# State-space scans on one Trainium2 core: the fourth channel block's input products by ScalarE and TensorE, and two of four scans in place in their PSUM banks

## The reference, cut to what matters

```python
def _mamba(x, in_w, conv_w, conv_b, xproj_w, dt_w, dt_b, A_log, D_param, out_w):
    xz = x @ in_w.T
    xh, z = jnp.split(xz, 2, axis=-1)
    ...                                  # causal conv of 4 taps, silu -> xc
    proj = xc @ xproj_w.T                # dt (16), Bm (16), Cm (16)
    delta = jax.nn.softplus(dt @ dt_w.T + dt_b)
    A = -jnp.exp(A_log)
    deltaA = jnp.exp(jnp.einsum('bld,dn->bldn', delta, A))
    deltaBu = jnp.einsum('bld,bln->bldn', delta * xc, Bm)
    def step(h, inp):
        dA, dBu, c = inp
        h = dA * h + dBu
        y = jnp.einsum('bdn,bn->bd', h, c)
        return (h, y)
    ...
    y = ys.transpose(1, 0, 2) + xc * D_param
    return (y * jax.nn.silu(z)) @ out_w.T
```

## Time and profile before

| | before |
|---|---|
| median of 3 runs | 5116.01 us (5112.91 to 5116.14) |
| profiled execution: its time, its span | 5119.58 us, 5117.9 us |
| mean granted TensorE clock | 0.935 |
| scans of all 16 halves | from 1144 to 2868 us of the span |
| busy in the whole span | PE 87%, DVE 68%, ACT 43%, POOL 48% |
| busy from 1253 to 2759 us (14 halves) | POOL 1431 of 1506 us, DVE 1354, PE 1245, ACT 855 |

### The profile page before, as it was taken

The page is one execution under the profiler, slowest core; times in us unless marked ns, Lnnn a source line. Parts: engine busy times, 40 slices in busy tenths (PEclk is TensorE's granted clock), DMA queues, the critical chain, the costliest instruction groups (busy, mean ns, idle before and its releaser), DMA issues. The chain is left out here.

```text
span 5117.9 us, 65289 instructions
## 1 busy us (share of the span) xinstructions
PE 4445.0 (87%) x22600; PEld 2900.7 (57%) x22600; DVE 3499.4 (68%) x7168; ACT 2189.7 (43%) x4132; POOL 2460.3 (48%) x1575
## 2 busy tenths in 40 slices
PE   7888599948888888888888799997898899999999
PEld 4555487623333333333333345796344799999998
DVE  4664222248988989889898574311896788888885
ACT  3555011125555555555555454333664233333332
POOL 3442400059999999999999441000122133222332
PEclk8998799969999999999999799998999899999999
DMA  2002213332222222222222100374000100000000
GB/s 73 1 1 97 79 52 109 100 99 70 70 70 70 68 68 70 69 70 70 69 70 70 39 1 7 132 263 159 1 1 18 71 5 3 5 5 5 5 5 5
DMA packets 153112, 287.22 MB, mean 56 GB/s; under 512 B 24441, under 2 KB 135024, under 8 KB 144206
## 3 DMA queue, kind: packets, MB, share of 16 engines
q1 hardware_dynamic: 144926, 263.59, 15.7%
q0 software_dynamic: 6656, 14.04, 0.9%
q10 hardware_dynamic: 1200, 5.42, 0.3%
HBM read 252.33 MB, written 33.42 MB: 56 GB/s over the span
## 5 line engine op out<-in xcount | busy, mean ns | idle before, releaser
L1734 PE MATMUL ssm_ps<-ssm_hc,net_ident 128*128 128x452 f32 x2048 | 950.8, 590 | 197.3 <-DVE ssm_hc L1990 105.4
L1916 POOL TENSOR_TENSOR ssm_dBu<-ssm_du,ssm_bc 128x904 f32<-128x904 f32 x512 | 1067.3, 2110 | 3.2 <-POOL ssm_du L1934 1.9
L1835 ACT ACTIVATE ssm_ps<-ssm_step,ssm_decay 128x448 f32<-128x448 f32 x1024 | 647.8, 636 | 651.1 <-DVE ssm_ps L1980 438.1
L1734 PEld LDWEIGHTS ssm_ps<-ssm_hc,net_ident 128*128 128x128 f32 x2048 | 387.9, 202 | 729.8 <-issue 341.3
L1980 DVE TENSOR_TENSOR_SCAN ssm_ps<-ssm_ps,ssm_dBu 128x452 f32<-128x452 f32 x512 | 565.2, 1104 | 132.9 <-POOL ssm_dBu L1916 46.0
L1980 DVE TENSOR_TENSOR_SCAN ssm_hs<-ssm_ps,ssm_dBu 128x452 f32<-128x452 f32 x512 | 551.4, 1077 | 40.2 <-ACT ssm_ps L1835 35.7
L1927 POOL TENSOR_TENSOR ssm_hc<-ssm_hs,ssm_bc 128x904 f32<-128x904 f32 x256 | 539.8, 2109 | 73.9 <-DVE ssm_hs L1980 73.8
L3170 POOL TENSOR_TENSOR peer_hid<-peer_hid,peer_weight 128x452 f32<-128x452 f32 x256 | 288.7, 1168 | 525.7 <-ACT peer_weight L3120 525.7
L3035 PE MATMUL peer_ps<-peer_xn,peer_down 128*128 128x226 f32 x2048 | 439.3, 361 | 0.0
L3101 PE MATMUL peer_ps<-peer_hid,peer_up 128*128 128x226 f32 x2048 | 398.8, 355 | 2.7 <-POOL peer_hid L3170 2.2
L3101 PEld LDWEIGHTS peer_ps<-peer_hid,peer_up 128*128 128x128 f32 x2048 | 388.2, 190 | 11.2 <-POOL peer_hid L3170 4.1
(11 more groups left out here) (425 smaller groups left out, 8000.9 us busy)
## 6 DMA issues: line engine op xcount, KB each, us to landing
ssm_bc<-ssm_rows SPq DMA_DIRECT2D x256, 452.0 KB, 3.6
l_ff_w<-in_l_ffn_w SPq DMA_DIRECT2D x64, 1024.0 KB, 6.7
moe_w_gu<-in_moe_gate_up SPq DMA_DIRECT2D x16, 704.0 KB
slots_in<-rt_zeros SPq DMA_DIRECT2D x17, 640.0 KB, 8.5
moe_rows_in<-slots_in SPq DMA_DIRECT2D x16, 512.0 KB
slots_out<-xp_rows_out SPq DMA_DIRECT2D x16, 512.0 KB
moe_w_dn<-in_moe_down SPq DMA_DIRECT2D x16, 384.0 KB
peer_down<-in_peer_down_t SPq DMA_DIRECT2D x1, 4096.0 KB, 16.3
```

The costliest lines, as they stand in the source:

```text
L1734: nc.tensor.matmul(Y_BANK[j][:, 0:GT], c["ident"][:, :], hc[:, q % 2, j, :], start=False, stop=(n == S - 1))\
L1835: nc.scalar.activation(rows(dA(i % 2))[:, :, lo:lo + N - 1], rows(step[hf.d][:, j, :])[:, :, lo:lo + N - 1], ACT.Exp, scale=decay[hf.d][:, ...
L1916: nc.gpsimd.tensor_tensor(dBu[:, q % 2, j:j + 2, :], du[hf.d][:, j:j + 2, :], bc[:, q % RING, 0:1, :].to_broadcast([P, 2, GT]), ALU.mult). ...
```

## The change

1. **Block 3's input products** leave POOL, for 15 of 16 states. The next half's B rows are turned once (tokens on partitions, `bT`, PE at slot 49 and ACT at slot 50), and so is block 3's `du` (`duT`, PE at slot 1, ACT at slot 3). Then ACT scales `duT` by a column of `bT`, one row of 113 tokens at a time (4 copies of 113x128 per state, `scaledT`), and PE turns the four results back into the bank `T_BANK`, which was `HS_BANK`. For n = 0 POOL still makes the product, in an instruction of its own (128x452), into `scaledT`. POOL's second input product is now block 2 alone (128x452).
2. **The scan of block 3** runs in place in `T_BANK` (for n = 0 in `scaledT`, in SBUF); its decays go to an SBUF tile, `dA_late`. **The scan of block 2** runs in place in its decay bank.
3. Since block 2's scan overwrites the zeros of bank 1, ACT zeroes them once a step with a small copy (`zeroed`), ahead of that slot's Exp.
4. `yz` now shares the buffer `conv`, with two new waits for that.

```diff
+    BT_MM, BT_OUT, DUT_MM, DUT_OUT = 49, 50, 1, 3
+    def turn_at(n):
+        return 6 if n == 1 else 50 if n == 12 else 4 * n + 1
+    def scale_at(n):
+        return (4, 4, 5, 5) if n == 1 else tuple(4 * n - 2 + b for b in range(4))
...
+        def dA(i):
+            return dA_late[:, :] if i % IB == LAST else A_BANK[i % 2][:, 0:GT]
+        def terms(hf, n, j):
+            q = S * hf.r + n
+            if j < LAST:
+                return dBu[:, q % 2, j, :]
+            return whole(hf, n) if n == 0 else T_BANK[:, 0:GT]
+        def late_state(hf, n, j):
+            return dA(AT[j]) if j < LAST else terms(hf, n, j)
...
+                    def turn_terms(hf, n):
+                        at = turned_before(hf, n)
+                        pe.wait_ge(s["hc_dve"], 2 * (S * hf.r + n))
...
+                        for b in range(GB):
+                            pe.wait_ge(s["scaled_done"], GB * (at - 1) + b + 1)
+                            mm = nc.tensor.transpose(T_BANK[:, b * N:(b + 1) * N], scaledT[0:N, n % 2, b, :], c["ident"][0:N, 0:N])
+                        mm.then_inc(s["turned_mm"], 1)
...
                     def decays(hf, i):
                         n, j = i // IB, ORDER[i % IB]
-                        if i >= 2:
-                            act.wait_ge(s["scan_done"], SLOTS * hf.r + i - 1)
+                        q = S * hf.r + n
+                        if i % IB == 1:
+                            if q:
+                                act.wait_ge(s["hc_dve"], 2 * q - 1)
+                            nc.scalar.activation(starts(i, hf.d), one[:, :].unsqueeze(1).to_broadcast([P, GB, 1]), ACT.Copy, scale=0.0)\
+                                .then_inc(s["zeroed"], 1)
+                        elif i == 0 or i == LAST:
+                            act.wait_ge(s["starts_zero"], 2 * hf.r + (1 if i == 0 else 2))
                         else:
-                            act.wait_ge(s["starts_zero"], 2 * hf.r + i + 1)
+                            act.wait_ge(s["scan_done"], SLOTS * hf.r + i - (3 if i % IB == LAST else 1))
...
+                                nc.scalar.activation(scaledT[0:N, n % 2, b, :], duT[:, b, :], ACT.Copy,
+                                                     scale=bT[:, hf.r % 2, b, n:n + 1]).then_inc(s["scaled_done"], 1)
...
-                        nc.gpsimd.tensor_tensor(dBu[:, q % 2, j:j + 2, :], du[hf.d][:, j:j + 2, :],
-                                                bc[:, q % RING, 0:1, :].to_broadcast([P, 2, GT]), ALU.mult).then_inc(s["dbu_done"], 1)
...
+                        nc.gpsimd.tensor_tensor(dBu[:, q % 2, 2, :], source[:, 2, :], row, ALU.mult).then_inc(s["dbu_done"], 1)
+                        if n == 0:
+                            if hf.r:
+                                pool.wait_ge(s["turned_mm"], turned_before(hf, 0))
+                            nc.gpsimd.tensor_tensor(whole(hf, 0), source[:, LAST, :], row, ALU.mult).then_inc(s["first_last"], 1)
...
                         if j >= 2:
-                            state = HS_BANK[:, 0:GT]
-                            if 2 * q + j - 2 > 0:
-                                dve.wait_ge(s["hc_dve"], 2 * q + j - 2)
+                            state = late_state(hf, n, j)
+                            if j == 2:
+                                dve.wait_ge(s["zeroed"], q + 1)
```

105 lines of the change are left out of this document (88 added, 17 removed).

## The result

The changed kernel takes 5080.40 us (median of 4 runs, 5077.52 to 5082.43), the kernel before 5116.08 beside it (4 runs, 5112.91 to 5119.00). The ratio is 0.9935, with a 95% interval of 0.9923 to 0.9947: faster by 36 us, where 50 were predicted. The profiled execution took 5081.52 us. Nearly the whole gain lies in the scans: in the profiled executions it is 1722.0 us from the start of the first to that of the last before, and 1687.1 after. Over the 14 middle halves a half takes 108.48 us before and 106.67 after. (My window of the earlier trace rows was 1506 us, a little less than the 1518.8 of 14 halves, so its figures per half were 0.8% low.)

A forecast was written before the change was run, and what follows sets the result against it. POOL and DVE were taken as near their limit in turn. Per half 4.6 + 1.4 - 0.5 - 0.7 - 1.7 = 3.1 us, 50 us in all, gave about 5070, or 5066 as median; own range 5026 to 5101, over all 4990 to 5128.

The forecast's parts named there:

- What bounds the kernel: POOL and DVE hand the limit back and forth; taking work from POOL alone returns at most 2.9 us a half.
- Own wait: Scans behind 23 of 32 DVE products a half stop waiting 0.20 us each: 4.6 us gained, bounds 0 and 7.
- POOL: DVE's waits for POOL shrink: 1.4 us a half gained, bounds 0 and 2.9.
- Slot 1: Where halves meet, POOL's product gets 0.9 to 1.0 us shorter; some 1.5 of the 2.5 us wait stays.
- The other waits: DVE's remaining waits for POOL, 2.9 - 2.5 = 0.4 us a half, go.
- ACT: Copies and zeroings raise ACT from 61 to about 83 of 104 us; -0.5 and +0.35 at SILU slots, put at 0.
- PE and the turn: Block 3's chain of product, add and turn has 1.1 us slack, broken at OUT_MM: 0.5 us a half lost.
- The signs to look for: In the profile after, new DVE waits for PE's turn appear in few slots (13 and 51), not every step.
- STEP: At slots 48 to 51 ACT stands behind B's turn with its copy and LOG; STEP about 0.7 us late.
- Two SBUF inputs: For n = 0, block 3's scan and product contend with POOL, 0.8 to 0.9 each: 1.7 us lost, bounds 0 and 4.2.
- In place: Scans reading and writing one bank: at most 0.03 x 31 = 0.9 us a half slower, taken as 0.

The follow-up runs named there:

- no_turn: The kernel before with only the scans of blocks 2 and 3 in place, nothing turned, POOL's work as before; 5071.21 us, ratio 0.9920.
- free_terms: no_turn with block 3's input products left out for all states but the first of a half; 5011.67 us, ratio 0.9791.
- wait_back: The changed kernel, but scans of blocks 2 and 3 again wait for the DVE product in front of them; 5133.05 us, ratio 1.0040.
- out_late: The changed kernel with output projections at slots 9 and 13, residuals and next half's first projections later too; 5088.75 us, ratio 0.9951.
- bt_in_xz: The changed kernel with B turned in the bank XZ at slot 47 instead of in T_BANK; 5091.31 us, ratio 0.9958.
- after_again: The changed kernel itself, timed once more beside no_turn on the same chip; 5083.34 us, ratio 0.9931.
- first_in_bank: The changed kernel with block 3's decays for n = 0 in T_BANK, so no DVE instruction has two SBUF inputs; 5072.79 us, ratio 0.9923.
- turn_first: The changed kernel with PE turning block 3's terms ahead of its slot's products, except at slots 5 and 49; 5089.40 us, ratio 0.9949.

## Why the prediction was right, and where its sum was not

**What bounds the kernel.** I named DVE and POOL and said that POOL's relief alone can return only DVE's 2.9 us a half. Once the own waits were gone, no_turn shows 66 us of waits for POOL in place of 40, and free_terms shows 62 us to be had. The bound was read from the kernel before and is too low for one in which DVE has become faster: I added two terms as if they stood apart.

**Own wait.** Right in mechanism and size: 0.74 to 0.51, -4.8 against -4.6, and wait_back loses 53 us, of which about 40 are this wait. The Trainium skill's rule ("VectorE: DVE Perf Modes", section "The DRAIN you can't avoid"), by which a semaphore between two operations of DVE costs nothing on top of the empty pipe, is not borne out here, by the traces and by wait_back. The same section says that a next operation that is not held starts earlier, and with that the trace agrees: 0.51 us after the start of a product that takes 0.60.

**POOL.** Slot 1 as predicted (-1.2 against -1.0). The other waits were mis-sized: 1.1 for 0.4. I had taken them as 2.9 of the groups of the earlier trace rows less 2.5, one half's wait at slot 1; over the 14 halves that wait is 2.3 on the average, and the groups count only idle time that they put down to POOL, while the spacings at slots 60 to 62 were 1.1 over the shortest. At slot 62 the profile puts them down to ACT.

**ACT.** Right at 0: slots 32 and 41 together 4.66 before, 4.63 after. The copies came 0.29 apart, as costed, and ACT grew to 1108 of 1482 us, 75%. It is a sum of two small moves, with the signs of the prediction but not its sizes: -0.16 at slot 32 (-0.5 expected) and +0.12 at slot 41 (+0.35).

**PE and the turn.** The step that failed. I saw the breach at OUT_MM only for the second projection (0.5). The rows at 2008 show it at the first: PE starts the eight passes just before block 3's product is ready, and add and turn stand behind all of them. That is 1.0 us a half at slot 11, where the sum had nothing, and 0.8 at slot 15 for the 0.5 of the second projection; out_late shows the cause of both. Slot 7, with 0.6 on top, was not foreseen either. It appears only in halves in which the mean clock of the 8 us before was 0.81 or less, behind 2.3 to 2.7 us in which PE idled; the prediction had priced the lower clock only for a chain that is late every step. So the term is 2.4 for 0.5. The signs to look for were named as slots 13 and 51: slot 13 is where PE makes the turn whose scan stands at slot 15, and at slot 51 only 0.1 was lost. The turn's own price (0.55 for four, 0.38 to the next instruction) was right.

**STEP.** Mechanism right, 1.2 for 0.7: bt_in_xz took it away by taking B out of the bank.

**Two SBUF inputs.** 2.0 for 1.7. A scan took up to 2.08 us (3.06 in after_again) and a POOL instruction 2.95; first_in_bank brought the scan back to 1.10. The Trainium skill's rule that the later of the two engines is held until the first is done ("SBUF — State Buffer", section "Who interferes with whom") agrees with the rows at 1463.64 and 1464.63.

**In place.** 0, and rather a gain of 0.007 us a scan.

**How near the sum came.** It had 3.1 us a half and 1.8 were measured. The turn, STEP and the two-input instructions cost 2.7 more than I had put, and the own wait, POOL and the rest gave 1.4 more than I had put. Half of the error cancelled, and that was luck.

**Where the rest of the gain went.** The prediction's sign rests on one of the change's two parts. The in-place scans bring all of it (no_turn); the turning earns 62 us from POOL and pays 69 in waits of its own. Each remedy took the wait that it aimed at away, and another came within some slots: ACT and PE work in order, and whatever is moved ahead there holds back something else, and where PE idles for it, it runs at the lower clock behind the pause in some halves. That ACT "has room on the average" (75%; PE 87%) was true of the sums and said little about the places.

## What to carry to other kernels

Before costing a relief, split the change in its parts and ask which of them would stand alone: here a short edit (results in place, so that no scan waits for the product in front of it on its own engine) has the whole gain. On engines that work in order, cost a new chain by what stands in front of it at each slot, and not by the engine's mean load. Split a wait's mean by halves and look at the granted clock beside it, before putting it down to the order of instructions. And if two engines hand the limit back and forth, work out their terms together, since the second is worth more once the first is taken.

## What was not expected of the hardware

- A wait of DVE for its own previous instruction costs 0.21 to 0.23 us each (0.74 against 0.51 from product to scan), though DVE runs in order anyway. In wait_back, with one wait more in front of block 2's scans, it is 0.28 (0.80); why was not tested.
- In turn_first the granted clock had a mean of 0.72 in the 6 us behind PE's 2.53 us of idle time, in the stretch shown; six passes took 3.56 us there for 2.45 elsewhere. After a like pause of 2.52 us in another half of the same execution it stayed at 1.00, and in the changed kernel, with a pause of 1.72, too. At a half's start in the changed kernel, a pause of 2.65 us was followed by 0.50 over 3.6 us (four passes in 3.38 us), and one of 2.68 by 1.00 (1.78 us).
- The turn of a 113x128 tile stands in the trace as one pass, and a product with the identity of the same type as two: four of the one took 0.38 us, eight 60-column ones of the other 1.92.
